# Graph network kernel: in each lap of fifteen message slots, TensorE builds one slot's node rows from one-hots instead of POOL gathering them; constant products in front of the last stage's waits

## The chip, the cores and the metric

One core of a Trainium2 chip runs the whole program. The metric is the device time of one execution in microseconds (us), smaller is better.

## The reference, cut to what matters

There are 6250 nodes with 64 features and 200000 edges sorted by destination. Two networks run one after the other, each behind a layer norm, a relu and an added residual. The second one holds the work that the change is about:

```python
msg_input = concatenate([node_feats[src], edge_sh, edge_radial], axis=-1)   # 64 + 9 + 8 columns
h = silu(msg_input @ W1 + b1)
h = silu(h @ W2 + b2)
messages = h @ W3 + b3
aggregated = segment_sum(messages, dst, num_segments=6250)
update_input = concatenate([node_feats, aggregated], axis=-1)
gate = sigmoid(update_input @ G + gb)
u = silu(layernorm(update_input @ U1 + ub1))
return node_feats + gate * layernorm(u @ U2 + ub2)
```

`node_feats[src]` takes, for each edge, the 64 float32 values of one node.

## The kernel before, in words

**Stages.** Up to about 1200 us the kernel makes the input rows and the first network: it counts edges between blocks of nodes (products of bf16 one-hots) and multiplies the 49 count blocks with node features that are split into three bf16 parts (`block_sums`, L768). Its last loop also writes the node features of the second network to a table in device memory (`m_tab`) and keeps them in SBUF (`hbuf`). Then comes the message stage, to about 3178 us, and the last stage (node update and output).

**Message stage.** The edges are cut into 391 slots of 512 edges (four tiles of 128). `LOOP` is 12: one lap of each engine's hardware loop holds 12 slots, and buffers go round in rings. For each slot:
- POOL (`gather_rows`, L633 to L641) issues four indirect DMAs, each for 128 rows of `m_tab` into `m_rows`, by indices in `m_idx`. It first waits until TensorE has turned the slot that held the same buffer one ring (12 slots) before, and, every second slot, for the indices (`idx_ready`).
- TensorE, in this order in step s: `turn_rows` (s), four transposes to features by edges (L928), then `hidden_in` (s-1), the product with W1 (L937), `hidden_out` (s-2) with W2 (L944), and `rows_back` (s-4), four products with W3 (L952). The waits name ScalarE's and DVE's semaphores of the slots before. A float32 product has two records in the trace.
- ScalarE copies the turned rows (L1282), makes both silus (L1288, L1293) and copies the output rows (L1300).
- DVE has one scan per slot (`scan_slot`, L2058), which adds up along the edges of a destination with a mask from SBUF and the terms from PSUM. In front of every second slot `next_idx` copies the next indices to `m_idx` (L2045).
- SP's queue (`move_slot`) loads attributes and the mask and stores the output rows.

Four DVE operations of the setup stage are named here because the prediction reads their durations: a cast of step numbers (L1556), a scaling that writes f16 (L1563), the subtraction of a per-partition number from the keys (L1582) and a shift of source numbers (L1579). So are the layer norm sums at L1528 and L1436, beside which POOL gathers rows of destinations (L580).

**Last stage.** When all output rows are stored, POOL gathers each node's last row in 49 indirect DMAs (L652), in nine groups of up to six. TensorE meanwhile multiplies the node features with `UGx` (`h_product`, L991), 49 tiles. For each group then: transposes of the gathered rows (`turn_agg`, L1003), a copy on ScalarE (`copy_agg`, L1372), the product with `UGa` (`agg_product`, L1012), the addition on DVE (L2080), layer norm by DVE and ScalarE, `turn_update` (L1022), silu, `update_out` (L1031), and the output arithmetic on DVE (L2124 to L2129). TensorE interleaves the group i's first two steps with group i-1's last two.

Of the kernel before, what the change touches and what calls it, by code (L numbers as in the profile page):

```python
# [28 lines left out]
LOOP = 12  # L29
# [6 lines left out]
MASK_RING = 6  # L36
ATTR_RING, TERM_RING, SCAN_RING, OUT_RING = 4, 3, 4, 4
HID_RING, BACK_RING = 2, 1
LAG = 4
EPAD = NB * BODY  # L40
# [68 lines left out]
def build(nc, x_in, dst_in, prev_in, first_in, src_in, rows_in, attr_in, w_in, v_in, out):  # L109
    with ExitStack() as ctx:  # L110
# [25 lines left out]
        src_all = sb("src_all", [P, ET + SLOTS * TB], I32)  # L136
# [57 lines left out]
        m_out = carve(slots_at, OUT_RING * TB * D).rearrange("p (k t f) -> p k t f", k=OUT_RING, t=TB)  # L194
        aggT = carve(2 * J * ROW, 2 * AGG_COLS, D).rearrange("p (k c) -> p k c", k=2)
# [46 lines left out]
        m_term = [ps[:, 2 + k, :] for k in range(TERM_RING)]  # L242
        m_back = [ps[:, 2 + TERM_RING, k * TB * D:(k + 1) * TB * D] for k in range(BACK_RING)]
# [107 lines left out]

        squares_summed = sem("squares_summed")
# [31 lines left out]
        rows_fetched = [sem(f"rows_fetched{i}") for i in range(len(END_GROUPS))]  # L384
# [12 lines left out]
        def _(sp):  # L397
# [105 lines left out]

            def load_hT(stores, groups):

                sp.wait_ge(m_stored, stores * DMA)
                sp.wait_ge(hT_stored, groups * DMA)
                sp.dma_start(hT, hT_d).then_inc(hT_loaded, DMA)

            def first_slots():  # L510
# [4 lines left out]
                for s in range(MASK_RING):  # L515
                    load_mask(s, s)

# [27 lines left out]
            with sp.Fori(1, LAPS - 1) as i:  # L545
                for k in range(LOOP):
                    move_slot(LOOP * i + k, k)
            for s in range(LOOP * (LAPS - 1), NSLOT):
# [10 lines left out]
        def _(pool):  # L559
# [73 lines left out]
            def gather_rows(i, k, tiles_of):  # L633
                if k % 2 == 0:
                    pool.wait_ge(e1.idx_ready, (LOOP // 2) * i + k // 2 + 1)
# [7 lines left out]
            with pool.Fori(0, LAPS - 1) as i:  # L643
                for k in range(LOOP):
# [13 lines left out]
        def _(pe):  # L658
# [37 lines left out]
            pe.sem_inc(e1.turn_done, ROW_RING)  # L696
            pe.wait_ge(loaded, LOADS * DMA)
# [223 lines left out]
            def turn_rows(s, k, lap, tiles_of=TB):  # L921

                pe.wait_ge(e1.gathered[k], DMA * (TB * lap + tiles_of))
# [5 lines left out]
                last.then_inc(e1.turn_done, 1)  # L929

# [25 lines left out]
            for k in range(LOOP):  # L956
# [5 lines left out]
                if k >= LAG:  # L962
                    rows_back(k - LAG, k - LAG, k - LAG >= BACK_RING)
            with pe.Fori(1, LAPS - 1) as i:
# [17 lines left out]

            def h_product(q):
# [419 lines left out]
        def _(dve):  # L1403
# [635 lines left out]
            dve.sem_inc(e1.idx_ready, LOOP // 2)  # L2039


            def next_idx(s, k):

                dve.wait_ge(e1.turn_done, s + 2 + ROW_RING)
                dve.tensor_copy(m_idx[:, k:k + 2, :].rearrange("p k t -> p (k t)"),  # L2045
                                src_all[:, bass.ds((s + LOOP) * TB, 2 * TB)]).then_inc(e1.idx_ready, 1)
# [14 lines left out]
            for k in range(LOOP):  # L2061
                if k % 2 == 0:
                    next_idx(k, k)
# [138 lines left out]
```

## Time and profile before

| | us |
|---|---|
| median of 3 runs | 3329.65 |
| lowest, highest | 3306.36, 3330.13 |
| the profiled execution's own time | 3333.66 |
| its span from the first to the last instruction | 3331.9 |
| mean granted TensorE clock, share of full | 0.865 |

The profile is of one execution. Busy times of POOL's indirect DMAs are those of the instruction that makes the transfers' descriptors, not of the transfers; the distance from one start to the next is the better measure.

### The profile page before, as it was taken

How to read it: one execution, taken by the hardware profiler on the slowest of the kernel's cores; microseconds unless marked ns; L12 is line 12 of the kernel's file. 1: busy time of each engine (PE TensorE's matmuls, PEld its weight loads, DVE VectorE, ACT ScalarE, POOL GpSimd, SP SyncE). 2: the span in 40 equal slices, each digit the busy share in tenths (PEclk: the TensorE clock that was granted, in tenths of full speed). 3: DMA queues.
4: the chain of work that ended last, by engine and by line, in shares of the span. 5: the costliest groups of instructions: out<-in, count | busy, mean ns of one | idle time of the engine just before them, and what ended most of it. 6: DMA issues, size and time to landing. Idle time of an engine off the chain costs nothing.

```text
span 3331.9 us, 54496 instructions
## 1 busy us (share of the span) xinstructions
PE 2636.7 (79%) x16695; PEld 1973.8 (59%) x16695; DVE 1446.8 (43%) x2038; ACT 1590.0 (48%) x2617; POOL 1564.0 (47%) x1663
## 2 busy tenths in 40 slices
PE   4599999859999957777777777777777777777786
PEld 3377777759989944444444444445444454454475
DVE  5999999863435532222222222222222222222226
ACT  2588888723332224444444444444444444444445
POOL 4000000000000037777777777777777777777750
PEclk9999999959999968888888888888888888888855
DMA  3133333419989944444444444444444444444410
GB/s 119 46 152 154 154 154 149 170 75 373 367 316 365 358 114 110 114 109 113 113 110 114 112 111 113 112 110 112 111 112 113 112 110 114 109 115 110 115 29 20
DMA packets 204366, 473.77 MB, mean 142 GB/s; under 512 B 48855, under 2 KB 100233, under 8 KB 185308
## 3 DMA queue, kind: packets, MB, share of 16 engines
q1 hardware_dynamic: 149973, 415.75, 36.0%
q0 software_dynamic: 53344, 55.75, 10.2%
q10 hardware_dynamic: 1001, 1.66, 0.1%
q8 instruction: 27, 0.44, 0.0%
q14 instruction: 21, 0.17, 0.0%
HBM read 336.57 MB, written 136.41 MB: 142 GB/s over the span
## 4 chain that ended last, share of the span: by engine, by line
POOL 40%; PE 28%; issue 16%; DVE 11%; DMA 3%; ACT 2%; POOLq 1%; DVEq 0%; ACTq 0%
POOL arena L639 39%; PE ps L768 13%; PE ps L787 6%; DMA arena<-m_tab,m_idx 2%; DVE arena L1845 2%; DVE stageT L1821 1%; PE ps L677 1%; PE ps L1012 1%; PE ps L944 1%; PE ps L952 1%; PE ps L937 1%; PE ps L991 1%; PE ps L928 1%; PE ps L665 1%; POOL arena L580 0%
## 5 line engine op out<-in xcount | busy, mean ns | idle before, releaser
L639 POOL DMA_INDIRECT arena<-m_tab,m_idx x1563 | 1478.5, 946 | 1617.0 <-issue 1609.7
L2058 DVE TENSOR_TENSOR_SCAN arena<-arena,ps 128x512 f32<-128x512 f32 x391 | 500.4, 1280 | 1434.1 <-ACT ps L1293 1261.6
L928 PE MATMUL ps<-ident,arena 128*64 128x128 f32 x1564 | 273.3, 305 | 481.1 <-DMA arena<-m_tab,m_idx 479.5
L952 PEld LDWEIGHTS ps<-weights,arena 128*128 128x128 f32 x3128 | 495.6, 226 | 256.6 <-issue 250.9
L944 PE MATMUL ps<-arena,weights 128*128 128x512 f32 x782 | 508.8, 739 | 0.0
L768 PE MATMUL ps<-arena 128*128 128x195 bf16 (+1 forms) x4802 | 481.4, 248 | 31.9 <-DVE arena L1787 31.3
L1282 ACT ACTIVATE arena<-ps 64x512 f32<-64x512 f32 x391 | 231.3, 591 | 564.1 <-PE ps L928 552.1
L928 PEld LDWEIGHTS ps<-ident,arena 128*64 128x64 f32 x1564 | 179.0, 133 | 514.8 <-issue 506.5
L937 PE MATMUL ps<-arena,weights 81*128 81x512 f32 x782 | 483.6, 705 | 0.2 <-ACT arena L1288 0.2
L952 PE MATMUL ps<-weights,arena 128*128 128x64 f32 x3128 | 461.5, 299 | 1.7 <-ACT arena L1300 1.7
L768 PEld LDWEIGHTS ps<-arena 128*128 128x128 f16 x4802 | 416.4, 98 | 62.7 <-DVE arena L1787 31.5
L1155 ACT ACTIVATE arena<-ps 128x588 f16<-128x588 f32 (+1 forms) x539 | 346.7, 644 | 107.3 <-PE ps L787 98.3
L1845 DVE TENSOR_TENSOR arena<-arena 128x2352 bf16<-128x2352 f16 (+1 forms) x294 | 351.4, 1224 | 16.5 <-PE ps L787 16.5
L1288 ACT ACTIVATE arena<-ps,weights 128x512 f32<-128x512 f32 x391 | 268.7, 687 | 187.5 <-PE ps L937 187.5
L1293 ACT ACTIVATE ps<-ps,weights 128x512 f32<-128x512 f32 x391 | 258.8, 662 | 169.2 <-PE ps L944 167.2
L944 PEld LDWEIGHTS ps<-arena,weights 128*128 128x128 f32 x782 | 179.1, 229 | 240.2 <-issue 237.5
L787 PE MATMUL ps<-arena 128*128 128x294 bf16 x1078 | 192.3, 297 | 34.8 <-DVE arena L1845 31.3
L1300 ACT ACTIVATE arena<-ps 128x256 f32<-128x256 f32 x391 | 150.3, 384 | 145.4 <-PE ps L952 145.4
L768 PE MATMUL ps<-wide,arena 128*128 128x192 bf16 x2401 | 205.7, 248 | 6.0 <-DMA arena<-count_d 3.2
L768 PEld LDWEIGHTS ps<-wide,arena 128*128 128x128 f16 x2401 | 201.6, 99 | 7.0 <-issue 3.5
L787 PE MATMUL ps<-arena,stageT 128*128 128x294 bf16 x1078 | 188.9, 293 | 0.5 <-ACT arena L1155 0.5
L787 PEld LDWEIGHTS ps<-arena 128*128 128x128 bf16 x1078 | 95.2, 99 | 89.8 <-DVE arena L1845 26.2
(264 smaller groups left out, 1800.1 us busy)
## 6 DMA issues: line engine op xcount, KB each, us to landing
arena<-count_d SPq DMA_DIRECT2D x98, 1568.0 KB, 8.5
arena<-keep_d SPq DMA_DIRECT2D x391, 256.0 KB
count_d<-arena SPq DMA_DIRECT2D x49, 1568.0 KB, 5.1
scan_rows<-arena SPq DMA_DIRECT2D x391, 128.0 KB
arena<-m_tab,m_idx POOLq DMA_INDIRECT x1563
arena<-attr_in SPq DMA_DIRECT2D x391, 34.0 KB
wide<-hT_d SPq DMA_DIRECT2D x1, 1617.0 KB
hT_d<-stageT ACTq DMA_DIRECT2D x12, 132.0 KB
```

Source lines behind the costliest of these rows:

```text
L639: pool.indirect_dma_start(m_rows[:, k, t, :], None, m_tab, bass.IndirectOffsetOnAxis(ap=m_idx[:, k, t:t + 1].bitcast(U32), axis=0))\
L768: last = pe.matmul(ps[:, bank, 0:rhs.shape[2]], blocks[block][:, a, :], rhs[:, a, :], start=(a == 0), stop=(a == J - 1), skip_group_check= ...
L787: last = pe.matmul(ps[:, bank, 0:WCOLS], hot_b[b][:, k % BATCH, :, i], hot_a[:, slot, k % UNIT, :, i], start=(i == 0), stop=(i == WT - 1))
L928: last = pe.transpose(m_turn[:, t * P:(t + 1) * P], m_rows[:, k, t, :], ident[:, :])
L937: pe.matmul(m_in, W("W1"), m_msg[:, k % ATTR_RING, :], start=True, stop=True).then_inc(e1.in_done, 1)
L944: pe.matmul(m_term[k % TERM_RING], W("W2"), m_hid[:, k % HID_RING, :], start=True, stop=True).then_inc(e1.w2_done, 1)
L952: last = pe.matmul(m_back[k % BACK_RING][:, t * D:(t + 1) * D], m_scan[:, k % SCAN_RING, t * P:(t + 1) * P], W("W3"), start=True, stop=True)
L1155: act.activation(blocks[r][:, :, 2 * m * WD:2 * m * WD + 2 * wd].rearrange("p a (w d) -> p a w d", w=2), ps[:, two:two + 2, 0:wd * J].rear ...
L1288: act.activation(m_hid[:, k % HID_RING, :], m_in, ACT.Silu, bias=W("b1")).then_inc(e1.silu1_done, 1)
L1293: act.activation(m_term[k % TERM_RING], m_term[k % TERM_RING], ACT.Silu, bias=W("b2")).then_inc(e1.silu2_done, 1)
L1845: dve.tensor_tensor(hot_a[:, u % HOT_SLOTS, 0:n, :, :], iota_w[:, :, :].unsqueeze(1).to_broadcast([P, n, WCOLS, WT]), keys, ALU.is_equal). ...
L2058: dve.tensor_tensor_scan(m_scan[:, k % SCAN_RING, :], m_mask[:, k % MASK_RING, :], m_term[k % TERM_RING], before, ALU.mult, ALU.add).then_ ...
```

## The change

`LOOP` goes from 12 to 15, so there are 27 laps and one slot in the last. In the 25 middle laps slot 14 (`PICKED`) is not gathered. SP broadcasts that slot's 512 source numbers to all partitions, DVE casts them to float32 (`know_pick`) and compares them with the node numbers of each of the 49 blocks of 128 nodes (`mark_pick`: 49 comparisons of 512 columns, float32 in, bf16 out, in nine bursts of six or five, one behind each of the scans of slots 0 to 8). TensorE multiplies each one-hot (four tiles of 128 edges) with the node table of that block in three bf16 parts (`pick_rows`: 196 products of 192 columns, in steps 5 to 13), and DVE adds the three parts into `m_rows` (`join_parts`). `split_nodes` makes the three-part table once, in the first lap. Index copies come every fifth slot. Rings change: masks from 6 to 5, attributes, scans and outputs from 4 to 5, hidden from 2 to 3.

In the last stage `keep_busy` puts products of a constant tile (128 x 128 by 256 columns, bf16), whose results nobody reads, in front of TensorE's waits: 32 ahead of `h_product`, then per group 8, 2, 4 and 2.

```diff
-LOOP = 12
+LOOP = 15
-MASK_RING = 6
-ATTR_RING, TERM_RING, SCAN_RING, OUT_RING = 4, 3, 4, 4
-HID_RING, BACK_RING = 2, 1
+MASK_RING = 5
+ATTR_RING, TERM_RING, SCAN_RING, OUT_RING = 5, 3, 5, 5
+HID_RING, BACK_RING = 3, 1
+IDX_STEP = 5
+PICKED = LOOP - 1
+PICKS = [(0, 6), (6, 6), (12, 6), (18, 6), (24, 5), (29, 5), (34, 5), (39, 5), (44, 5)]
+PICK_RING, PICK_BLOCKS, PICK_LAG = 3, 6, 5
...
+            def load_pick(lap):
+                sp.dma_start(pick_int, src_row[:, bass.ds((LOOP * lap + PICKED) * BE, BE)].partition_broadcast(P)).then_inc(pick_loaded, DMA)
...
-            with pool.Fori(0, LAPS - 1) as i:
-                for k in range(LOOP):
+            for k in range(LOOP):
+                gather_rows(0, k, TB)
+            with pool.Fori(1, LAPS - 1) as i:
+                for k in range(PICKED):
                     gather_rows(i, k, TB)
...
+            def pick_rows(lap, n):
+
+                pe.wait_ge(pick_ready, len(PICKS) * (lap - 1) + n + 1)
+                pe.sem_inc(alone, 1)
+                first, blocks = PICKS[n]
+                for a in range(first, first + blocks):
+                    for t in range(TB):
+                        last = pe.matmul(ps[:, 3 + TERM_RING + t // 2, (t % 2) * PARTS * D:(t % 2 + 1) * PARTS * D],
+                                         pick[:, n % PICK_RING, a - first, t * P:(t + 1) * P],
+                                         node_parts[:, a, :, :].rearrange("p q d -> p (q d)"),
+                                         start=a == 0, stop=a == J - 1, skip_group_check=True)
+                last.then_inc(pick_used, 1)
...
                     turn_rows(s, k, i)
+                    if PICK_LAG <= k < PICK_LAG + len(PICKS):
+                        pick_rows(i, k - PICK_LAG)
                     hidden_in(s - 1, (k - 1) % LOOP, i if k >= 1 else i - 1)
...
+            flat = ones[:, :].bitcast(BF16)
+
+            def keep_busy(bank, n):
+
+                for _ in range(n):
+                    pe.matmul(ps[:, bank, 0:2 * P], flat[:, 0:P], flat[:, :], start=True, stop=True)
...
-                pe.wait_ge(rows_fetched[i], n * DMA)
                 if i >= 1:
                     pe.wait_ge(agg_copied, i)
                 else:
                     pe.wait_ge(h_kept, KEEP_UNITS)
+                keep_busy(3, 8)
+                pe.wait_ge(rows_fetched[i], FETCHED + n * DMA)
...
-                pe.wait_ge(agg_copied, i + 1)
                 if i >= 1:
                     pe.wait_ge(u_ready, i)
+                keep_busy(0, 2)
+                pe.wait_ge(agg_copied, i + 1)
...
-                pe.wait_ge(u_staged, i + 1)
                 if i >= 1:
                     pe.wait_ge(u_done, i)
+                keep_busy(5, 4)
+                pe.wait_ge(u_staged, i + 1)
...
-                pe.wait_ge(u_done, i + 1)
                 if i >= 1:
                     pe.wait_ge(v_added, i)
+                keep_busy(7, 2)
+                pe.wait_ge(u_done, i + 1)
...
+            keep_busy(6, 32)
             for q in range(KEEP_UNITS):
                 h_product(q)
...
+            def split_nodes(n):
+
+                q = n // 2
+                if n > 0:
+                    dve.wait_ge(nodes_split, n)
+                of = hbuf if q == 0 else ybuf
+                if n % 2 == 0:
+                    dve.tensor_copy(node_parts[:, :, q, :], of[:, :, :]).then_inc(nodes_split, 1)
+                else:
+                    dve.tensor_tensor(ybuf[:, :, :], of[:, :, :], node_parts[:, :, q, :], ALU.subtract).then_inc(nodes_split, 1)
+
+            def know_pick(lap):
+
+                dve.wait_ge(pick_loaded, DMA * lap)
+                dve.tensor_copy(pick_src, pick_int).then_inc(pick_known, 1)
+                dve.wait_ge(pick_known, lap)
+
+            def mark_pick(lap, n):
+
+                dve.wait_ge(pick_used, len(PICKS) * (lap - 1) + n + 1)
+                first, blocks = PICKS[n]
+                for a in range(first, first + blocks):
+                    last = dve.tensor_scalar(pick[:, n % PICK_RING, a - first, :], pick_src, node_no[:, a:a + 1], None, ALU.is_equal)
+                last.then_inc(pick_ready, 1)
+
+            def join_parts(lap):
+
+                dve.wait_ge(pick_used, PICK_RING + len(PICKS) * lap)
+                for n in range(2):
+                    last = dve.tensor_reduce(m_rows[:, PICKED, 2 * n:2 * n + 2, :], m_pick[n].rearrange("p t q d -> p t d q"), AX.X, ALU.add)
+                last.then_inc(picked, 1)
...
                 for k in range(LOOP):
-                    if k % 2 == 0:
-                        next_idx(LOOP * i + k, k)
+                    if k == 0:
+                        know_pick(i)
+                    if k == PICK_LAG + len(PICKS) - 3:
+                        join_parts(i)
+                    if k % IDX_STEP == 2:
+                        next_idx(LOOP * i + k - 2, k - 2)
                     scan_slot(LOOP * i + k, k, i)
+                    if k < len(PICKS):
+                        mark_pick(i, k)
```

## Rows read from the trace of the kernel before

**Rows 1.** Page: span, POOL and the granted clock in 40 slices, chain by line
```profile
span 3331.9 us, 54496 instructions
...
POOL 4000000000000037777777777777777777777750
PEclk9999999959999968888888888888888888888855
...
POOL arena L639 39%; PE ps L768 13%; PE ps L787 6%; DMA arena<-m_tab,m_idx 2%; DVE arena L1845 2%; DVE stageT L1821 1%; PE ps L677 1%; PE ps L1012 1%; PE ps L944 1%; PE ps L952 1%; PE ps L937 1%; PE ps L991 1%; PE ps L928 1%; PE ps L665 1%;
```

**Rows 2.** POOL by line, 1200 to 3250 us (busy us, mean ns | idle before)
```profile
L639 POOL DMA_INDIRECT arena<-m_tab,m_idx x1563 | 1478.5, 946 | 1617.0 <-issue 1609.7 <-PE ps L928 6.4 <-DVE m_idx L2045 0.9
L652 POOL DMA_INDIRECT ybuf<-scan_rows,end_idx x49 | 46.8, 955 | 34.1 <-DMA scan_rows<-arena 19.5 <-issue 14.6
```

**Rows 3.** Busy us of PE, PEld, DVE, ACT, POOL; clock; DMA share
```profile
2200.00:2700.00 500.00, 381.31 (x1600) 246.38 (x1600) 132.06 (x150) 231.96 (x400) 377.99 (x401) 0.84 0.46 112
...
3200.00:3250.00 50.00, 39.58 (x137) 34.58 (x136) 13.00 (x20) 22.34 (x28) 32.62 (x35) 0.50 0.12 23
```

**Rows 4.** TensorE timeline in the message stage (start us, us, line, shapes, count)
```profile
2012.59 1.02 PE L937 MATMUL ps<-arena,weights 81*128 81x512 f32 x2
...
2015.59 1.02 PE L937 MATMUL ps<-arena,weights 81*128 81x512 f32 x2
...
2020.85 0.60 PE L928 MATMUL ps<-ident,arena 128*64 128x128 f32 x4 [2.54 <-DMA arena<-m_tab,m_idx]
```

**Rows 5.** DVE by line in the message stage, 1250 to 3100 us
```profile
L2058 DVE TENSOR_TENSOR_SCAN arena<-arena,ps 128x512 f32<-128x512 f32 x369 | 472.3, 1280 | 1359.0 <-ACT ps L1293 1186.7 <-PE ps L952 163.6 <-issue 8.7
```

**Rows 6.** TensorE timeline, 49 products of 192 columns, 1124 to 1130 us
```profile
1124.12 4.21 PE L768 MATMUL ps<-wide,arena 128*128 128x192 bf16 x49
1128.16 1.03 PE L819 MATMUL ps<-weights,stageT 128*128 128x64 f32 x8
```

**Rows 7.** DVE timeline in the setup: operations with one source
```profile
75.26 0.29 DVE L1556 CAST stage<-arena 128x256 bf16<-128x256 int32 x1 [0.24 <-DVE hbuf L1552]
...
79.52 0.47 DVE L1563 TENSOR_SCALAR arena<-arena 128x588 f16<-128x588 int32 x1
...
83.44 0.35 DVE L1582 TENSOR_SCALAR ends<-ends,win_base 110x256 f32<-110x256 f32 x1
83.71 0.29 DVE L1579 TENSOR_SCALAR arena<-wide 110x256 int32<-110x256 int32 x1
```

**Rows 8.** Timelines of DVE and of POOL, 19 to 28 us
```profile
19.55 3.43 DVE L1528 TENSOR_TENSOR ybuf<-xres,mean 128x3136 f32<-128x3136 f32 x1
23.01 3.42 DVE L1436 TENSOR_TENSOR arena<-ybuf 128x3136 f32<-128x3136 f32 x1
...
20.42 3.44 POOL L580 DMA_INDIRECT arena<-dst_in,win_int  x1 [0.31 <-issue]
24.16 3.16 POOL L580 DMA_INDIRECT arena<-dst_in,win_int  x1 [0.30 <-issue]
27.62 1.01 POOL L580 DMA_INDIRECT arena<-dst_in,win_int  x1 [0.30 <-issue]
```

**Rows 9.** Timelines of two index copies on DVE, one beside its gather
```profile
1467.22 0.14 DVE L2045 COPY m_idx<-src_all 128x8 int32 x1
...
1572.46 0.94 POOL L639 DMA_INDIRECT arena<-m_tab,m_idx  x1 [0.30 <-issue]
1573.09 0.31 DVE L2045 COPY m_idx<-src_all 128x8 int32 x1
```

**Rows 10.** Last stage: TensorE timeline, and the chain by line from 3180 us
```profile
3178.35 31.67 PE L991 MATMUL ps<-weights,wide 66*128 66x192 f32 x98
...
3212.95 4.20 PE L1012 MATMUL ps<-weights,arena 64*128 64x192 f32 x12 [0.89 <-ACT arena L1372]
...
3221.69 4.21 PE L1012 MATMUL ps<-weights,arena 64*128 64x192 f32 x12 [3.12 <-ACT arena L1372]
...
by line: PE ps L1012 22.8%; PE ps L991 19.4%; PE ps L1031 6.6%; DVE arena L2080 4.8%; ACT L1365 4.2%; ACT arena L1372 4.1%; issue 3.7%; PE ps L1022 2.9%; DVE var L2102 2.6%; ACT stageT L1380 2.4%; DVE ybuf L2125 2.4%; DVE ybuf L2128 2.4%; D
```

More of the change, by code:

```diff
@@ L106, with build @@
 V_TOTAL = _at
-def build(nc, x_in, dst_in, prev_in, first_in, src_in, rows_in, attr_in, w_in, v_in, out):
+def build(nc, x_in, dst_in, prev_in, first_in, src_in, src_row, rows_in, attr_in, w_in, v_in, out):
     with ExitStack() as ctx:
@@ L135, in build @@
         upto = sb("upto", [P, P])
-        src_all = sb("src_all", [P, ET + SLOTS * TB], I32)
+        src_all = sb("src_all", [P, ET + LOOP * TB], I32)
         xres = sb("xres", [P, J, D])
@@ L194, in build @@
         m_out = carve(slots_at, OUT_RING * TB * D).rearrange("p (k t f) -> p k t f", k=OUT_RING, t=TB)
+        slots_at += OUT_RING * TB * D
+        pick = carve(slots_at, PICK_RING * PICK_BLOCKS * BE // 2).bitcast(BF16).rearrange("p (k a e) -> p k a e", k=PICK_RING, a=PICK_BLOCKS)
+        slots_at += PICK_RING * PICK_BLOCKS * BE // 2
+        pick_int, pick_src = carve(slots_at, BE).bitcast(I32), carve(slots_at + BE, BE)
+        node_parts = ends[:, :, :].rearrange("p j f -> p (j f)")[:, 0:J * PARTS * D // 2].bitcast(BF16)\
+            .rearrange("p (a q d) -> p a q d", a=J, q=PARTS)
         aggT = carve(2 * J * ROW, 2 * AGG_COLS, D).rearrange("p (k c) -> p k c", k=2)
@@ L242, in build @@
         m_term = [ps[:, 2 + k, :] for k in range(TERM_RING)]
+        m_pick = [ps[:, 3 + TERM_RING + n, 0:2 * PARTS * D].rearrange("p (t q d) -> p t q d", t=2, q=PARTS) for n in range(2)]
         m_back = [ps[:, 2 + TERM_RING, k * TB * D:(k + 1) * TB * D] for k in range(BACK_RING)]
@@ L349, in __init__ @@
                 self.stored = [sem(f"m_stored{k}") for k in range(OUT_RING)]
+        pick_loaded, pick_known, nodes_split, pick_ready, pick_used, picked = (sem(n) for n in (
+            "pick_loaded", "pick_known", "nodes_split", "pick_ready", "pick_used", "picked"))
         squares_summed = sem("squares_summed")
@@ L383, in build @@
         agg_turned, agg_copied, agg_multiplied = (sem(n) for n in ("agg_turned", "agg_copied", "agg_multiplied"))
-        rows_fetched = [sem(f"rows_fetched{i}") for i in range(len(END_GROUPS))]
+        rows_fetched = e1.gathered[1:1 + len(END_GROUPS)]
+        FETCHED = DMA * TB * (LAPS - 1)
         u_ready, u_squared, u_staged, u_turned, u_done, gate_done, v_done, v_added, v_squared = (sem(n) for n in (
@@ L516, in first_slots @@
                     load_mask(s, s)
+                load_pick(1)
             sp.wait_ge(way_known, 1)
@@ L544, in _ @@
                 move_slot(k, k)
-            with sp.Fori(1, LAPS - 1) as i:
+            with sp.Fori(1, LAPS - 2) as i:
                 for k in range(LOOP):
                     move_slot(LOOP * i + k, k)
-            for s in range(LOOP * (LAPS - 1), NSLOT):
+                sp.wait_ge(pick_known, i)
+                load_pick(i + 1)
+            for s in range(LOOP * (LAPS - 2), NSLOT):
                 move_slot(s, s % LOOP)
@@ L633, in gather_rows @@
             def gather_rows(i, k, tiles_of):
-                if k % 2 == 0:
-                    pool.wait_ge(e1.idx_ready, (LOOP // 2) * i + k // 2 + 1)
+                if k % IDX_STEP == 0:
+                    pool.wait_ge(e1.idx_ready, (LOOP // IDX_STEP) * i + k // IDX_STEP + 1)
                 pool.wait_ge(e1.turn_done, LOOP * i + k + 1)
@@ L696, in _ @@
             pe.sem_inc(e1.turn_done, ROW_RING)
+            pe.sem_inc(pick_used, PICK_RING)
             pe.wait_ge(loaded, LOADS * DMA)
@@ L921, in turn_rows @@
             def turn_rows(s, k, lap, tiles_of=TB):
-                pe.wait_ge(e1.gathered[k], DMA * (TB * lap + tiles_of))
+                if k == PICKED and not isinstance(lap, int):
+                    pe.wait_ge(picked, lap)
+                else:
+                    pe.wait_ge(e1.gathered[k], DMA * (TB * lap + tiles_of))
                 if not isinstance(lap, int) or s >= 1:
@@ L963, in _ @@
                     rows_back(k - LAG, k - LAG, k - LAG >= BACK_RING)
+            pe.wait_ge(nodes_split, 2 * PARTS - 1)
             with pe.Fori(1, LAPS - 1) as i:
@@ L2192 @@
               "first_in": np.ascontiguousarray(dst[::P]).reshape(1, ET),
-              "src_in": np.concatenate([src.reshape(ET, P).T, np.zeros((P, SLOTS * TB), i32)], axis=1),
+              "src_in": np.concatenate([src.reshape(ET, P).T, np.zeros((P, LOOP * TB), i32)], axis=1),
+              "src_row": src.reshape(1, EPAD),
               "rows_in": np.ascontiguousarray(rows).reshape(EROWS, 2 * P), "attr_in": attr, "w_in": w, "v_in": v}
```

16 lines of the change are left out of this document (9 added, 7 removed).

## Prediction

> **What bounds the kernel now.** I read the page first, then the chain, then POOL by line, then windows. In 40 slices POOL has work from slice 15 to 38 without a break, and the chain that ended last has 39% of its time in one POOL line, L639, the indirect DMAs that gather source rows [rows 1]. POOL's group has 1563 of them with 946 ns busy each; the idle time ahead is "issue" for all but 7 us [rows 2]. The stretch from 2200 to 2700 us holds 401 gathers in 500 us, 1.25 us from start to start [rows 3]. So POOL never waits for anyone: the message stage costs 1563 x 1.25 = 1954 us, a slot of four gathers 5.0 us. TensorE is busy for 381 of those 500 us at a granted clock of 0.84 [rows 3], but waits for the gathers: at the upper clock a slot takes it 3.00 us (2012.59 to 2015.59), then it stands 2.54 us for a gather [rows 4]. DVE has one scan of 1.28 us in a slot and waits for ScalarE [rows 5]. Behind the gathers comes a last stage of 155 us, TensorE at a clock of 0.50 [rows 3].
>
> **Gathers removed.** 25 middle laps lose one slot of four gathers: 100 x 1.25 = 125 us off POOL, all of it on the path. POOL's wait for a turned slot gets no nearer: it reuses a buffer 15 slots old.
>
> **TensorE's added work** has 196 products of 192 columns per lap. In the first network 49 such products run from 1124.12 to 1128.16 us, 82 ns each [rows 6]; so 16.1 us per lap at the upper clock. With 15 x 3.00 that is 61 us, against 14 x 5.0 = 70 us of POOL. In the nine steps with picks TensorE needs 3.0 + 1.8 = 4.8 us, inside POOL's 5.0, and 15 buffers lie between them. Cost 0, if the clock holds; otherwise it is a rival below. The join (two reductions) falls into step 13 behind the last pick, with three products' worth of other work ahead of the turn of slot 14: 0. SP's 256 KB broadcast of numbers is queued behind slot 14's loads and is needed some three slots later: 0; the late masks (ring 5) are still loaded a slot ahead, three slots before their scan: 0. Uncovered, either would cost a transfer of some us per lap once, up to 25 x 3 = 75.
>
> **DVE's added work.** One comparison has one source, 512 columns, and a per-partition number. A scaling of 588 columns to f16 took 0.47 us, a cast of 256 to bf16 0.29 [rows 7]: 0.52 ns per column, so 0.43 us for 512, and the per-partition number adds 0.06 (0.35 against 0.29 at 256 columns [rows 7]): 0.49 us. Unlinked operations start sooner than the one before ends: 83.44 to 83.71, 0.08 less than its 0.35 [rows 7]. So 0.41 us apart, a burst of six 2.5 us, 49 of them 20.1 us per lap. With 15 scans (19.2) and some 2 us of casts and joins DVE has 41 of 70 us, and a slot with a burst 3.8 of 5.0. That hides, since the scan stands three term buffers behind. But they are one-source operations between SBUF tiles like the index copies, and this matters to POOL.
>
> **What the comparisons do to the gathers** is the largest term, and no row shows it as such. The nearest rows: a gather that started at 20.42, while DVE was in a 3.43 us operation with two SBUF sources, took 3.44 us in place of 1.01, until 0.88 us behind DVE's end; the next one, at 24.16, took 3.16 us in the same way [rows 8]. So a gather that starts within such an operation is held until 0.13 us before its reported end, and then does all its work. The other way round, an index copy of 0.14 us that started 0.63 us into a gather took 0.31 us and ended with it [rows 9]; of 192 index copies the 39 that start 0.55 to 0.78 us into a gather are all stretched so, and the 51 that start at 0.05 to 0.50 take 0.14 or 0.15. So a gather has two stops at something that it shares with DVE's fast one-source operations: one at its start, and one from 0.52 to 0.79 us in. If a comparison holds it as the long ones do, it holds for 0.49 - 0.13 = 0.36 of each 0.41 us.
> By averages: a stop meets a hold with chance 0.36/0.41 and waits 0.18 us, 0.16 per stop, 0.32 per gather. A gather holds DVE for 0.33 us in turn, so the bursts take 25 us of a lap, with 16 gathers: 5.1 us per lap, 128 in 25 laps. By rhythm: a first stop that is let go at the end of a comparison puts the second one (0.52 us on, behind one more comparison) 0.3 us ahead of an end, and that one the next first stop again 0.3; so 0.16 + 0.30 + 0.30 = 0.76 per burst, 225 bursts, 171 us. I take 140, nearer to the average, since a burst starts when ScalarE's silu is done and keeps no step with POOL. Lower end 0 (the comparisons share nothing with the gathers; a gain has no cause). Upper end: the hold isn't let go between unlinked comparisons; a burst of 2.25 us less 0.3 until the first stop, 1.93 x 225 = 434 us.
> The Trainium skill ("SBUF — State Buffer", SBUF: two separate sides) says that DVE in a two-port mode and GpSimd exclude each other for a whole instruction, and that GpSimd then can't write descriptors. The gathers beside the long operations agree; that page speaks against this change, and by it the hold would be near the two counts above, by its absence 0.
>
> **Once and small.** The table is split in the first lap: three casts of 3136 columns (1.76 us each by the rate above) and two operations of 3.43 us. Each holds POOL about once: 2.4 and 2.2 as in the rows [rows 8], some 1.2 for each cast, 8 us. 25 casts of numbers: 1 us. Bounds 0 and 12.
>
> **The last stage.** TensorE runs at the lower level (1.2 GHz, clock 0.50 [rows 3]); `h_product` takes 31.7 us without a pause, and from 3180 us the chain (152 us) has 22.8% in L1012, 19.4% in L991, 6.6% in L1031, 2.9% in L1022 [rows 10]: 79 us. At 2.4 GHz half of it goes, 39 us, less the products in front. One of these is 256/192 of 82 ns, 0.11 us at the upper level and 0.22 at the lower; 32 are 3.5 or 7 us. So the best is -36. If the clock stays down: 7 us, and per group 16 x 0.22 = 3.5 us, of which the pauses ahead of L1012 (0.89 or 3.12 us [rows 10]) hide one to three: +12, together +19. `h_product` alone, busy all along, did not raise the clock [rows 10], and the constant products are a tenth to a quarter of a group's time; but they are of full width. I take -8, the middle.
> The Trainium skill ("TensorE: Matmul & The Clock Gate", What's actually happening) says that sustained activity releases the throttle. The row of `h_product` disagrees, as narrow float32 products filled 31.7 us at the lower level; by the page alone this term would be near -36.
>
> **Sum.** From the profiled execution's own time: 3333.7 - 125 + 140 + 9 - 8 = 3350. Its time is 4.0 above the median of the runs, so 3346 in runs. The change gives with one hand and takes with the other: no difference that a measurement shows (about 1% is what it can tell from none here). With the hold between 92 and 200 and the end between -30 and +10, this case spans 3276 to 3420.
>
> **Rivals.**
> 1. Only the first stop is held, or the comparisons hold far shorter than their reported time: 16 x 0.16 x 25 = 64 by averages, 36 by rhythm, 50 taken: 3256. For it: index copies, of the same kind, never made a gather longer (their mean is 946 ns [rows 2]). Against: they are of 8 elements, with 0.02 us of hold by the rule above.
> 2. No hold at all, the change does what it says: 3206. For it: scans beside gathers cost them nothing. Against: a scan has one SBUF source at normal speed.
> 3. TensorE becomes the bound: at the 0.84 of [rows 3] its lap is 61/0.84 = 73 us, above 70, so 25 x 3 = 75 us come back, 3281. It can only decide where POOL is held by less than 3 us a lap. Against: a TensorE with less idle time has no cause for a lower clock.
> 4. Slower, by one mechanism: the hold is kept through a burst of unlinked comparisons in `mark_pick`, 434 us: 3640. The point from which it makes the kernel slower is a hold of 125 + 9 - 8 = 126 us, 0.56 us per burst. For it: the comparisons overlap in their reported times [rows 7]. Against: the gather of 20.42 got in between two long operations only 0.03 us apart [rows 8], though these were linked by a semaphore.
>
> **Chances.** Forecast 0.50, of which 0.05 faster by over 1%, 0.25 within, 0.20 slower; rival 1 0.25 (0.22 faster); rival 2 0.10, faster; rival 3 0.05 (0.04 faster); rival 4 0.08, slower; other ways to be slower (a late scan or load) 0.02. Faster 0.41, within 1% 0.29, slower 0.30. The range reaches down to rival 2 with a good last stage left out, 3200, and up to 3430, the forecast's upper bound; rival 4 stays out.
>
> **What would show it.** 1463 gathers in the page. Gathers in steps with bursts longer than 0.95 us or in two sizes, those outside at 0.95: their mean about 1.05 (140/1463 more). Comparisons of 0.49 us, some stretched to 0.8 by a gather. Picks 82 ns apart. A stretch of 500 us in the middle with some 370 gathers. Clock in the last stage 0.5, or above 0.8 if the constant products work. Wrong if gathers stay at 0.95 us beside comparisons (then 3206 to 3256), or if TensorE's idle time in the message stage goes to nothing.

## The result, and the profile after

The changed kernel took 3273.15 us (median of four runs, 3264.46 to 3290.56) beside 3319.45 for the kernel before on the same chip (four runs, 3306.36 to 3330.13): ratio 0.986, 95% interval 0.982 to 0.990, 46 us faster. The forecast was 3346. The profiled execution took 3278.17 us, 55.5 less than that of before.

The page after: span, POOL and granted clock in 40 slices, chain by line.
```profile
span 3276.4 us, 66009 instructions
...
POOL 4000000000000027777777777777777777777750
...
PEclk9999999969999978999999999999999999999987
...
POOL arena L659 39%; PE ps L791 14%; PE ps L810 6%; DVE arena L1899 2%; PE ps L964 2%; DVE stageT L1875 1%; DMA arena<-m_tab,m_idx 1%; PE ps L991 1%; PE ps L976 1%; PE ps L983 1%; PE ps L1063 1%; PE ps L699 1%; PE ps L954 1%; PE ps L1040 0%; PE ps L687 0%
```
The gathers still set the pace [rows 1], but TensorE's granted clock is 0.9 or more in all but the first slice of the message stage, where it was 0.8.

POOL and DVE by line in the message stage (busy us, mean ns | idle before), and the busy times of one stretch (PE, PEld, DVE, ACT, POOL; clock, DMA).
```profile
L659 POOL DMA_INDIRECT arena<-m_tab,m_idx x1463 | 1474.2, 1008 | 1578.9 <-issue 1570.1 <-PE ps L954 7.3 <-DVE m_idx L2099 1.5
...
L2124 DVE TENSOR_SCALAR arena<-arena,node_no 128x512 bf16<-128x512 f32 x1212 | 503.1, 481 | 0.0
...
L2109 DVE CAST ends<-ybuf 128x3136 bf16<-128x3136 f32 x2 | 6.8, 3393 | 0.0
...
2200.00:2700.00 500.00, 448.03 (x2962) 335.00 (x2961) 271.96 (x470) 237.33 (x410) 383.86 (x382) 0.95 0.48 116
```
There are 1463 gathers of 1008 ns in place of 1563 of 946 [rows 2]: each is 62 ns longer, 91 us in all. POOL still waits for nobody, and makes 382 gathers in 500 us in place of 401 [rows 3].

Timelines of POOL and DVE around one slot with a burst.
```profile
2209.23 0.94 POOL L659 DMA_INDIRECT arena<-m_tab,m_idx  x1 [0.31 <-issue]
2210.47 0.94 POOL L659 DMA_INDIRECT arena<-m_tab,m_idx  x1 [0.30 <-issue]
2211.72 1.24 POOL L659 DMA_INDIRECT arena<-m_tab,m_idx  x1 [0.30 <-issue]
2213.27 0.94 POOL L659 DMA_INDIRECT arena<-m_tab,m_idx  x1 [0.30 <-issue]
...
2210.69 2.16 DVE L2124 TENSOR_SCALAR arena<-arena,node_no 128x512 bf16<-128x512 f32 x5
```
The comparisons start at 2210.69 and every 0.4 us from there. The gather of 2211.72 starts inside one and takes 0.30 us longer; the gather of 2210.47, under way when the burst starts, keeps its 0.94.

Where the 55.5 us are. The starts of the first and of the last gather of source rows, in the timelines of POOL, cut the two profiles in three:

| stretch | before | after | difference |
|---|---|---|---|
| to the first gather | 1207.2 | 1199.8 | -7.4 |
| first to last gather | 1953.9 | 1918.9 | -35.0 |
| last gather to the end of the span | 170.7 | 157.7 | -13.1 |

The first stretch is not the change's: four runs of the experiments below start their first gather at 1184.7 to 1207.3 us, with the same code ahead of it. The second is 100 gathers less, -125.0, and 90.0 us on top. Counted over all gathers of the trace as time above 944 ns (what an undisturbed one takes here; 946 in the kernel before, so some 3 us go the other way), the 505 gathers that run beside a comparison add 86.8 us, and two that the long subtractions of the first lap held (3.02 and 3.72 us) add 4.9. So some 87 us are the bursts'. In the third stretch the last stage itself, counted from POOL's first gather of end rows, got 17.2 us shorter (150.3 to 133.1), and the way from the last gather of source rows to that point 4.1 us longer (20.4 to 24.5).

TensorE's timeline around one burst's products:
```profile
3121.03 1.81 PE L964 MATMUL ps<-ends,arena 128*128 128x192 bf16 x20
3122.68 1.05 PE L976 MATMUL ps<-arena,weights 81*128 81x512 f32 x2
```
Twenty picks in 1.65 us are 82 ns each, as in the first network [rows 6].

TensorE's timeline in the last stage, and the clock by stretch.
```profile
3140.70 5.77 PE L1030 MATMUL ps<-ones 128*128 128x256 bf16 x32
3146.31 16.09 PE L1040 MATMUL ps<-weights,wide 66*128 66x192 f32 x98
...
3165.79 2.21 PE L1063 MATMUL ps<-weights,arena 64*128 64x192 f32 x12 [0.67 <-ACT arena L1426]
...
3148.00:3165.00 17.00, 16.20 (x105) 15.65 (x103) 0.00 (x0) 9.81 (x14) 12.76 (x14) 1.00 0.13 27
...
3210.00:3250.00 40.00, 31.75 (x184) 26.81 (x184) 25.49 (x48) 22.41 (x30) 0.00 (x0) 0.79 0.04 16
3250.00:3276.00 26.00, 12.07 (x56) 9.20 (x55) 17.32 (x46) 13.99 (x22) 0.00 (x0) 0.58 0.09 32
```
`h_product` takes 16.1 us in place of 31.7 and the group's product 2.21 in place of 4.20 [rows 10]; the clock is 1.00 at first and falls to 0.58 at the end, where it was 0.50 throughout.

### The profile page after: what moved, and what is told of

Same layout as the page of the kernel before. It is cut to its first block, busy times and chain, and to the rows that moved or that the text cites. A ratio compares the mean times of both kernels' runs of the same rounds, so it can differ in the third digit from the quotient of the medians.

```text
span 3276.4 us, 66009 instructions
## 1 busy us (share of the span) xinstructions
PE 2835.2 (87%) x21771; PEld 2262.9 (69%) x21771; DVE 1975.1 (60%) x3229; ACT 1589.0 (48%) x2617; POOL 1559.3 (48%) x1563
## 4 chain that ended last, share of the span: by engine, by line
POOL 39%; PE 30%; issue 15%; DVE 11%; DMA 2%; ACT 2%; POOLq 1%; DVEq 0%; ACTq 0%
POOL arena L659 39%; PE ps L791 14%; PE ps L810 6%; DVE arena L1899 2%; PE ps L964 2%; DVE stageT L1875 1%; DMA arena<-m_tab,m_idx 1%; PE ps L991 1%; PE ps L976 1%; PE ps L983 1%; PE ps L1063 1%; PE ps L699 1%; PE ps L954 1%; PE ps L1040 0%; PE ps L687 0%
## 5 line engine op out<-in xcount | busy, mean ns | idle before, releaser
L659 POOL DMA_INDIRECT arena<-m_tab,m_idx x1463 | 1474.2, 1008 | 1578.9 <-issue 1570.1
L991 PEld LDWEIGHTS ps<-weights,arena 128*128 128x128 f32 x3128 | 433.7, 201 | 207.6 <-issue 204.8
L2124 DVE TENSOR_SCALAR arena<-arena,node_no 128x512 bf16<-128x512 f32 x1225 | 508.5, 481 | 0.0
L791 PEld LDWEIGHTS ps<-arena 128*128 128x128 f16 x4802 | 417.1, 98 | 63.0 <-DVE arena L1841 31.7
L964 PE MATMUL ps<-ends,arena 128*128 128x192 bf16 x4900 | 459.1, 252 | 0.0
L954 PE MATMUL ps<-ident,arena 128*64 128x128 f32 x1564 | 250.1, 285 | 226.9 <-DMA arena<-m_tab,m_idx 223.9
L976 PE MATMUL ps<-arena,weights 81*128 81x512 f32 x782 | 434.8, 639 | 0.2 <-ACT arena L1342 0.2
L983 PE MATMUL ps<-arena,weights 128*128 128x512 f32 x782 | 430.8, 633 | 0.0
L964 PEld LDWEIGHTS ps<-ends,arena 128*128 128x128 bf16 x4900 | 426.9, 100 | 5.5
L991 PE MATMUL ps<-weights,arena 128*128 128x64 f32 x3128 | 411.4, 277 | 1.7 <-ACT arena L1354 1.7
L954 PEld LDWEIGHTS ps<-ident,arena 128*64 128x64 f32 x1564 | 167.1, 124 | 250.4 <-issue 246.9
L983 PEld LDWEIGHTS ps<-arena,weights 128*128 128x128 f32 x782 | 158.3, 203 | 204.6 <-issue 203.9
```

The source lines that it names most:

```text
L659: pool.indirect_dma_start(m_rows[:, k, t, :], None, m_tab, bass.IndirectOffsetOnAxis(ap=m_idx[:, k, t:t + 1].bitcast(U32), axis=0))\
L791: last = pe.matmul(ps[:, bank, 0:rhs.shape[2]], blocks[block][:, a, :], rhs[:, a, :], start=(a == 0), stop=(a == J - 1), skip_group_check= ...
L954: last = pe.transpose(m_turn[:, t * P:(t + 1) * P], m_rows[:, k, t, :], ident[:, :])
L964: last = pe.matmul(ps[:, 3 + TERM_RING + t // 2, (t % 2) * PARTS * D:(t % 2 + 1) * PARTS * D], pick[:, n % PICK_RING, a - first, t * P:(t ...
L976: pe.matmul(m_in, W("W1"), m_msg[:, k % ATTR_RING, :], start=True, stop=True).then_inc(e1.in_done, 1)
L983: pe.matmul(m_term[k % TERM_RING], W("W2"), m_hid[:, k % HID_RING, :], start=True, stop=True).then_inc(e1.w2_done, 1)
```

## The experiments

Theory A: comparisons hold the gathers, the hold is what eats most of the 125 us that the change could give, and it is smaller than forecast because most of it is a gather's first stop. Rivals: TensorE, 448 of 500 us busy, takes part of it; or the constants give more than -13 and something else loses.

**The constants alone gone.**
```diff
             def keep_busy(bank, n):
-                for _ in range(n):
-                    pe.matmul(ps[:, bank, 0:2 * P], flat[:, 0:P], flat[:, :], start=True, stop=True)
+                return
```


> The changed kernel without the constant products in the last stage. Theory (they raise the clock): from the last gather of the message stage to the end 171 to 177 us in place of 157.7, TensorE's granted clock there back to 0.50, h_product 31.7 us in place of 16.1; the whole 13 to 18 us longer than the changed kernel, so a ratio of about 0.990 to the kernel before. Rival (the last stage moved by chance, the constant products give nothing): clock and time as in the changed kernel, within 5 us.

Measured 3285.06 beside 3313.98 for before on that chip: 0.992 (0.988 to 0.996). The clock by stretch of its last stage:
```profile
3160.00:3283.00 123.00, 81.34 (x297) 68.19 (x296) 63.08 (x127) 63.33 (x85) 25.69 (x27) 0.50 0.08 21
```
From the last gather to the end it takes 173.2 us in place of 157.7, so the constants are worth 15.5 us between these two profiles, and the rest of the gain is the gathers'. The size is rough: the three kernels below that keep the constants on this kind of chip take 149.5, 155.0 and 155.6 us there, so by them it is 18 to 24. `h_product` is again at the lower level, for 31.1 us without a pause; in the changed kernel the granted clock went to its upper level near the end of the 5.8 us of constant products, and `h_product` ran in 16.1. Which of their properties does it, the width or the type, no run separates.

**The comparison in the form that also sums its columns**, same output.
```diff
-dve.tensor_scalar(pick[...], pick_src, node_no[:, a:a + 1], None, ALU.is_equal)
+dve.tensor_scalar(pick[...], pick_src, node_no[:, a:a + 1], 0.0, ALU.is_equal, ALU.add,
+                  accum_out=mean[:, a:a + 1])
```


> The changed kernel with the comparisons in the form that also sums up its output (same one-hots, the sum is not used). Theory (two-port operations hold the gathers): this form runs one column per cycle, about 0.8 us apart by the searches of the setup, and takes no second port; gathers back at a mean of 0.95 us in place of 1.008, the two long subtractions excepted, so about 75 to 80 us less than the changed kernel: ratio to before about 0.962. Rival A (any DVE operation of one source holds them, by its length): mean of the gathers above 1.05 us, slower than the changed kernel. Rival B (DVE becomes the bound: 49 x 0.8 + 15 x 1.28 + 3 = 61 us of a lap of 70, in nine steps 5.5 us of 4.7): gathers wait for turned slots, POOL's idle time shows TensorE or DVE as the releaser, time between the two.

Measured 3183.55, ratio 0.960 (0.955 to 0.966). POOL and DVE by line:
```profile
L659 POOL DMA_INDIRECT arena<-m_tab,m_idx x1463 | 1386.5, 948 | 1586.4 <-issue 1576.6 <-PE ps L954 8.8 <-DVE m_idx L2099 0.9
...
L2124 DVE TENSOR_SCALAR_CACHE_REDUCE arena<-arena,node_no 128x512 bf16<-128x512 f32 x1225 | 828.9, 737 | 0.0
```
DVE starts the comparisons 0.67 us apart in place of 0.40, and yet the gathers are back at 948 ns: the hold goes with the form of the instruction, not with DVE's load. This settles theory A: the stage is 1831 us, 87.6 less than in the changed kernel, with all picks, constants and new rings still there, so none of these was in the way. On this kind of chip it beats both kernels, as the halves below do with the same output. The Trainium skill ("SBUF — State Buffer", Who interferes with whom) has just this: the fast form takes the ports that DVE shares with GpSimd, the form that also writes its accumulator does not. The runs agree.

**Fewer comparisons**: one per burst, 9 of 49, so slot 14 gets the rows of other nodes; TensorE's work is whole.
```diff
-                                         pick[:, n % PICK_RING, a - first, t * P:(t + 1) * P],
+                                         pick[:, n % PICK_RING, 0, t * P:(t + 1) * P],
...
-                for a in range(first, first + blocks):
+                for a in range(first, first + 1):
                     last = dve.tensor_scalar(pick[...], ...)
```


> Leaves out 40 of the 49 comparisons of a lap (each burst makes only its first block's one-hot, and TensorE uses it for all blocks of the burst; 196 products stay). Theory (hold per comparison): the gathers' excess over 0.946 us falls from 88 us to some 23 (8 of it from the two long subtractions), 65 us less than the changed kernel, ratio about 0.966. Rival (TensorE becomes the bound when POOL is free: 61 us at full clock of a lap of 70): less than 30 us gained, TensorE without idle time in the message stage.

Measured 3182.55, 0.962 (0.957 to 0.967); mean gather 954 ns. The gathers beside a comparison add 7.9 us in place of 86.8; 15 were expected (23 less 8 for the subtractions), so sign and place are right and the size is off by a factor of two. This run shows the first stop by itself. Of the gathers that start 80 ns or more into a comparison of 0.46 us, 42 are held, and all go on 0.33 us into it, 0.125 to 0.131 ahead of its reported end: just what [rows 8] gave for an operation seven times as long. An estimate by averages comes near here: 225 comparisons x 0.33 x 0.33 / (2 x 1.25) = 9.8 us.

**Each comparison as two of 256 columns**, same output.
```diff
+                    for b in range(2):
+                        half = slice(b * BE // 2, (b + 1) * BE // 2)
-                    last = dve.tensor_scalar(pick[..., :], pick_src, ...)
+                        last = dve.tensor_scalar(pick[..., half], pick_src[:, half], ...)
```


> Each comparison as two of 256 columns. By what remains of one operation when a gather starts: operations 0.35 us long, 0.27 apart, a hold of 0.22 us: a first stop waits 0.09 us on average in place of 0.16, so the excess of the gathers falls from 88 to 50 to 60 us, 30 us less than the changed kernel. By the port's total time (98 x 0.22 = 21.6 us per lap against 49 x 0.36 = 17.6): excess 100 us or more, not faster.

Measured 3189.56, 0.961 (0.956 to 0.966), mean gather 951 ns; the gathers beside a comparison add 4.3 us. Both figures expected for this run (50 to 60, or 100 and more) missed by a factor of ten or more, with the subtractions' share taken off. The cause is in the phases, counted over all gathers of the trace (ns from the start of the comparison in which the gather starts; extension over 944 ns; phases with few gathers left out):

| changed kernel, 512 columns | gathers | mean extension | halves, 256 columns | gathers | mean extension |
|---|---|---|---|---|---|
| 0 to 40 | 21 | 53 | 0 to 40 | 479 | 1 |
| 80 to 160 | 256 | 285 | 80 to 160 | 27 | 94 |
| 240 to 280 | 12 | 164 | 240 to 280 | 71 | 0 |
| 360 to 400 | 7 | 58 | | | |

The left side shows both stops: a gather that starts 80 ns or more into a comparison of 0.48 us is let go about 0.35 us into it where it meets the first stop alone, and ends as if let go at 0.43 to 0.45 where it meets the second one too. But where in the comparison it starts is no matter of chance. Of the halves, one that starts 0.50 to 0.55 us into a gather takes 544 ns in place of 340 (402 of them), so the next two start at 0.98 and 1.24 us, and the next gather, at 1.25, comes within 40 ns of a start and is not held.

**Three pieces** of 176, 176 and 160 columns test this: a rhythm makes shorter pieces worse again.

> The changed kernel with each comparison cut in three (176, 176 and 160 columns), same output. From 0.396 and 0.26 us apart for 512 and 256 columns they should be 0.22 us apart. Theory of the rhythm: a comparison that starts 0.50 to 0.72 us into a gather is stopped until about 0.72, so the following ones start at about 0.94 and 1.16, and the next gather at 1.25 falls some 0.1 us into one that lets go at 0.18: 0.08 us for each of some 675 gathers beside bursts, excess of the gather stage over 1.25 us a gather some 54 us (25 to 90), well above the 4.9 us of the halves although the pieces are shorter; time about 3240 us, ratio 0.977. Rival (the shorter the piece, the less a gather waits): excess below 10 us, time about 3190 us, ratio 0.962.

This run and all that follow were on chips of another kind, on which the kernel before takes 4145 to 4203 us (below), so the time tells nothing of the hold: ratio 1.081 (1.077 to 1.086), and 1.089 (1.084 to 1.094) when it was run again. The gathers beside bursts do. From POOL's timeline of the repeated run:
```profile
1412.00 1.10 POOL L659 DMA_INDIRECT arena<-m_tab,m_idx  x1 [0.30 <-issue]
1413.41 1.10 POOL L659 DMA_INDIRECT arena<-m_tab,m_idx  x1 [0.30 <-issue]
1414.81 1.11 POOL L659 DMA_INDIRECT arena<-m_tab,m_idx  x1 [0.30 <-issue]
1416.22 0.94 POOL L659 DMA_INDIRECT arena<-m_tab,m_idx  x1 [0.30 <-issue]
```
Of the gathers that start within a piece, 286 of 309 do so 80 to 120 ns into it, where 0.1 us was predicted, and are held 0.111 us on average (0.08 predicted); in sum 34 us for all gathers beside comparisons. In their usual phase pieces a third shorter than the halves hold a gather 111 ns in place of 1. The rhythm is confirmed per gather; the 54 us of the whole stage were not reached, as 427 gathers ran beside bursts and not the 675 counted on.

**The constants elsewhere.** Three kernels: before with the constants alone, the summing form without them, and the changed kernel with only the 32 ahead of `h_product`.

> The kernel before, with the constant products of the last stage and nothing else of the change. Theory (the constants themselves lift TensorE's clock in the last stage): from the last gather of source rows to the end some 156 us in place of 170.8, the 98 records of h_product in some 16 us in place of 31.7, time about 15 us less than before, ratio 0.995. Rival (it is the picks that keep TensorE warm up to the last stage, and the constants only add work): h_product stays at some 31 us, the last stage is as long as before or up to 8 us longer, ratio 1.000 to 1.003.

> The changed kernel with the comparisons in the form that also sums its columns, and without the constant products. Theory (the parts add up, and the constants are worth 15 us wherever they stand): 3183.6 + 15 = 3199 us, ratio 0.965, from the last gather to the end some 173 us. Rival (with TensorE at 0.95 of its clock in the message stage the last stage starts warm without them): 3184 us, ratio 0.960.

> The changed kernel with only the 32 constant products in front of h_product; those in each group are gone. Theory (the 32 lift the clock for h_product, which gives 15 us for their 6, and the ones in the groups keep it up for another 4 to 6): from the last gather to the end 162 to 164 us (157.7 with all, 173.2 with none), h_product in 16 us, time about 3278 us, ratio 0.989. Rival A (the 32 do it all, and those of the groups cost as much as they give): 157 us, 3273 us. Rival B (those of the groups carry the gain): above 168 us, h_product at 31 us or its gain given back behind.

All three were on the other kind of chip: ratios 0.999 (0.997 to 1.002), 1.095 (1.090 to 1.099) and 1.069 (1.065 to 1.074), and when run again 1.001, 1.109 and 1.076. As tests of the constants by time they are inconclusive. TensorE by line in the last stage can still be read, first before with the constants, then with only the 32:
```profile
L1021 PE MATMUL ps<-weights,arena 64*128 64x192 f32 x98 | 24.5, 411 | 17.1 <-ACT arena L1384 17.1
```
```profile
L1061 PE MATMUL ps<-weights,arena 64*128 64x192 f32 x98 | 34.4, 535 | 19.9 <-ACT arena L1422 19.9
```
A group's products take 411 ns with all constants (438 when run again), though nothing was picked, 535 with only the 32, and 539 in the kernel before. So the constants lift the clock without the picks, and for the groups it is those in the groups that do it. The 32 alone, which take 5.3 us, make `h_product` busy for 27.1 and 26.1 us where it is 33.1 without any constants on this kind of chip; as it stands still in between for reasons of that chip, what they are worth elsewhere stays open.

**The other kind of chip: the changed kernel itself, fewer products, fewer of both.** The second has pick_rows multiply the first block of each burst alone (36 of 196 products per lap), the third makes only that block's comparison as well; slot 14 then gets the rows of nine blocks.
```diff
                 first, blocks = PICKS[n]
-                for a in range(first, first + blocks):
+                for a in range(first, first + 1):
                     for t in range(TB):
                         last = pe.matmul(...)
```


> The changed kernel as it is, on this call's chip. If that chip is of the kind on which ScalarE stands still at three places of each lap (the kernel before at some 4150 to 4200 us): ratio 1.07 to 1.09, the three places at slots 1, 6 and 11 of the lap with 12 to 20 us of distance between output copies in place of 5. If it is of the other kind: ratio 0.986 again.

> The changed kernel in which TensorE multiplies only the first block of each burst (36 of 196 products per lap; slot 14 gets rows of nine blocks only, so the output isn't the reference's); the comparisons are whole. Where ScalarE stands still in each lap. Theory (the standing is the supply of instructions, and 160 products with their weight loads make it longer): the lap falls from 117 us to some 95 to 100, ratio 0.96 to 0.99. Rival (it depends on the lap's length alone, or on the comparisons): within 2% of the changed kernel on the same chip. On a chip without the standing: within 1% of the changed kernel, since TensorE isn't the bound, unless the clock falls.

> As the run before, and DVE makes only the comparison of the first block of each burst (9 of 49). Where ScalarE stands still: by the theory of the instructions another 40 instructions less of DVE, so at most 5 us per lap under the run before; by the rival that the comparisons are what stands in the way, most of the loss comes back here. On the other kind of chip: excess of the gather stage under 10 us, ratio 0.96.

Measured beside 4200.25 us for before: the changed kernel 4503.09, 1.072 (1.068 to 1.075); fewer products 4058.68, 0.968 (0.964 to 0.972); fewer of both 4271.7, 1.016 (1.014 to 1.018). Waits of the engines in the changed kernel, and a piece of its timeline, of ScalarE and TensorE:
```profile
POOL arena L659 <- DVE m_idx L2099: 1028.4, 64, 31.9
ACT arena L1342 <- remote: 753.1, 83, 21.5
...
ACT arena L1354 <- remote: 464.4, 87, 12.8
...
PE ps L964 <- issue: 448.6, 485, 3.2
...
2243.29 0.38 ACT L1354 ACTIVATE arena<-ps 128x256 f32<-128x256 f32 x1 [2.33 <-remote]
2246.12 0.59 ACT L1336 ACTIVATE arena<-ps 64x512 f32<-64x512 f32 x1 [2.45 <-remote]
...
2254.67 0.48 PE L964 MATMUL ps<-ends,arena 128*128 128x192 bf16 x2 [1.09 <-issue]
...
2256.09 0.32 PE L964 MATMUL ps<-ends,arena 128*128 128x192 bf16 x1 [0.94 <-issue]
...
2257.51 0.48 PE L964 MATMUL ps<-ends,arena 128*128 128x192 bf16 x2 [1.11 <-issue]
...
2263.89 0.69 ACT L1342 ACTIVATE arena<-ps,weights 128x512 f32<-128x512 f32 x1 [17.18 <-remote]
```
"remote" is a wait whose end no event of this core explains. ScalarE stands in such waits for up to 21 us at a time and SP's queue for 1286 us in all. TensorE doesn't wait for them: from 2244 to 2265 us it makes its products a few at a time, and its picks one or two, with about 1 us in between in which it waits for nothing that the profile shows ("issue"; ahead of picks 485 times, 449 us in all; on the first kind of chip this line has no idle time at all). POOL goes on until it has used up its indices, and then waits for the next index copy, which comes behind DVE's waits for ScalarE (64 times, 1028 us). Within one execution the places are the same in most laps: from output copy to output copy a slot takes 5 us, but 24.5, 18.8 and 15.5 us (medians) behind slots 1, 6 and 11 of the changed kernel. In the kernel before with constants they are behind slots 3, 7 and 11 in one profile (11.1, 12.9 and 11.5 us) and behind others in the second, so the place isn't the code's alone. The lap is 119 us in place of 74, and 84 in place of 60. Transfers are hardly slower there: a 2048-byte packet of SP's queue takes 123 ns and 116 on average, a load of 1568 KB lands after 8.5 us on both.

Engines that make their instructions one by one with nothing to wait for, longer with more instructions in the body, fit the supply of instructions to the engines; 320 instructions less on TensorE (160 products with their weight loads) made the lap 19 us shorter (119 to 100) and the change a gain again, as the first theory said. But 40 comparisons less on DVE made it 10 us longer (109), which neither theory has. And the profile's own record of instruction loads speaks against it, as far as that record is complete: the changed kernel has 30 and 22 packets on the two instruction queues on both kinds of chip, and on this one none of them between 1500 and 4300 us, where the stops are. So the products are shown to cost time there; that it is by instruction supply is only argued, and why the third kernel loses is open.

## Why the prediction was wrong

- **Gathers removed, -125:** right, 100 gathers at 1.25 us.
- **The hold, +140: this is the step that failed**, and in it the second stop and the holding share. The forecast had two stops of 0.16 us for each gather, or 0.16 + 0.30 + 0.30 per burst. Measured: some 87 us, 0.39 per burst of 225. The first stop was read rightly: the 72 gathers that met it alone were held 0.242 us on average, where the law taken from [rows 8] gives 0.237 for their phases, and by this law the first stop makes about 63 of the 87 us. That the forecast's average gave 64 for it is luck, since 256 of the 335 gathers that start in a comparison do so within the same 80 ns. The second stop costs about 0.08 us where it meets a comparison, not 0.16 to 0.30, and makes some 24 us together with the few long holds below, not 64 or more. That mechanism was read rightly in [rows 9], but of an index copy beside a gather: DVE waits for the gather there, not the gather for DVE. The forecast turned a row that shows DVE's loss into a loss of POOL. "Keeps no step with POOL" was wrong as well: the gathers and the comparisons make each other wait and fall into step, and the step decides the sum. An average over phases is then no estimate; at 256 columns it would have been off by ten.
- **Split, +9:** 4.9 for the subtractions (4.6 forecast). The casts were forecast at 1.76 us and to hold some 1.2 each; they took 3.39, 1.08 ns per column, the rate of a two-source operation, and held nothing. The gather of 1239.81 ran beside one in 0.94 us.
- **Last stage, -8:** -13.1. The middle between the bounds -36 and +19 was too careful by 5 us. The clock did rise, not to the end of the stage: the stage itself lost 17.2 us, and 4.1 of them were given back between the last gather and the first end gather, as TensorE was further behind.
- **TensorE and DVE, 0:** right, with 448 and 272 of 500 us busy; picks 82 ns apart, comparisons 481 ns against 490 forecast. The clock rose to 0.95 with the picks, so rival 3 had no ground.
- **Rivals.** The first (only the first stop, 3256) came nearest, 17 us below what came, but its condition doesn't hold: the second stop exists, and the hold is 87 us where it had 50; the first and last stages made up for part of that. The second (no hold, 3206) is what the summing form shows. The fourth (hold kept through a burst) exists for single gathers. In the changed kernel 2 of 1463 took 2.4 us, with the constants gone 7 took 2.4 to 3.0, and with fewer products, on the other kind of chip, 46 took 2.0 to 2.8 and were held for 59 us in all. One of these, beside its burst:
```profile
1622.21 2.54 POOL L659 DMA_INDIRECT arena<-m_tab,m_idx  x1 [0.31 <-issue]
...
1622.59 2.04 DVE L2124 TENSOR_SCALAR arena<-arena,node_no 128x512 bf16<-128x512 f32 x5
```

The burst starts 0.38 us into the gather, and the gather ends 0.12 us behind the burst. What makes these few last is open.

- In the profile's own time the forecast was 72 us too high: 59 in the gather stage, 5 in the last stage, and 7 from the first stages, whose length differs from run to run.
- **Not seen at all:** on the other kind of chip the change makes the kernel 7% slower (one chip; on a second one the changed kernel itself was not timed, but three kernels made from it are 7 to 11% slower). The statement that the changed kernel is faster holds for the kind of chip on which both were first timed.

## What to carry to other kernels

Before giving DVE fast one-source work beside POOL's indirect DMAs, try the form that also sums: each instruction was 0.26 us longer, and the gather stage 88 us shorter. Where two engines stop each other at fixed points of short periodic instructions, look for the rhythm rather than an average: a gather that started in a comparison was held 250 ns on average by wholes, 7 by halves and, on the other kind of chip, 106 by thirds (235 by wholes there). And when instructions are what a change adds, 196 products in a loop body here, time it on more than one chip: the summing form, 4% faster than the kernel before on the first kind, is 9 to 11% slower than it on the other (there without the constants).

## What was not expected of the hardware

- The hold runs both ways with different rules. A gather that starts 80 ns or more into a fast comparison waits until 0.13 us ahead of its reported end, one that starts in the first 40 ns hardly does (halves: 1 ns for 479 of them; wholes: 53 ns for 21). DVE waits only when a comparison starts 0.50 to 0.75 us into a gather: of the halves' 402 that start at 0.50 to 0.55 the mean is 544 ns in place of 340, of those that start at 0.75 and later about 330. The Trainium skill's page named above lets one side have the ports for its whole instruction; most holds measured here are shorter at both ends, and a few last through a whole burst.
- A cast of 128 x 3136 float32 to bf16 took 3.39 us, as long as a subtraction of the same size and twice what the rate of the short ones gives (0.42 us for 512 columns from int32, 0.29 for 256 [rows 7]). The short ones write a contiguous row, this one 64 columns of every 192; no run tests whether that is the cause.
- The granted clock of a last stage with many short waits was 0.50 throughout without constant products, and 1.00 at first and 0.58 at the end with 5.8 us of them ahead of it and some in each group.
